# Adding transfers into the result in DRAM in place of loaded partial sums, in a two-layer graph kernel

## What is computed

```python
h = relu(layernorm(x));  h = h @ W0 + B0
mask = (adj < 0.5) & ~eye
S = where(mask, exp(-(1/adj - 1/mu)**2 / (2*sigma**2)), 0)
x = x + S @ h                       # layer 1
h = relu(layernorm(x)) @ W1.T
x = x + (adj*adj + eye) @ h         # layer 2; x is the result
```

## Time and profile before

| | |
|---|---|
| median of 3 runs | 1907.28 us |
| the profiled execution, its own time | 1907.14 us |
| its span, first to last instruction | 1905.3 us |
| TensorE busy | 1850.5 us (97%) |
| VectorE busy | 1732.5 us (91%) |
| ScalarE busy | 1733.1 us (91%) |
| DMA, mean | 521.19 MB, 274 GB/s |
| transfers of GpSimd's queue | 196, 51.39 MB |

### The profile page before, as it was taken

One profiled execution on the slowest core, in us unless ns is written; L12 is line 12 of the kernel. 1 busy time (PEld: TensorE's weight loads), 2 busy tenths in 40 slices (PEclk: granted clock), 3 DMA queues, 4 the chain that ended last, 5 costly groups with the idle time before them and its releaser, 6 DMA issues.

```text
span 1905.3 us, 13395 instructions
## 1 busy us (share of the span) xinstructions
PE 1850.5 (97%) x4820; PEld 886.4 (47%) x4820; DVE 1732.5 (91%) x1024; ACT 1733.1 (91%) x986; POOL 111.6 (6%) x201
## 2 busy tenths in 40 slices
PE   6989999999999999999999999999999999999997
PEld 4544443444444444444444444444444445555554
DVE  7999999998999999999999999999999955678776
ACT  7999999898999999999999999999999988777552
POOL 0000001100000000000000000000000000000112
PEclk9999999999999999999999999999999999999999
DMA  7576887797868687767776686666566577667995
GB/s 264 204 287 255 317 306 278 302 342 284 346 240 337 252 320 283 279 253 276 269 272 241 264 307 238 255 242 231 227 231 226 198 277 279 270 247 302 338 372 229
DMA packets 84289, 521.19 MB, mean 274 GB/s; under 512 B 11008, under 2 KB 11392, under 8 KB 28032
## 3 DMA queue, kind: packets, MB, share of 16 engines
q1 hardware_dynamic: 68544, 468.94, 64.6%
q0 software_dynamic: 15680, 51.39, 7.4%
HBM read 492.50 MB, written 27.79 MB: 273 GB/s over the span
## 4 chain that ended last, share of the span: by engine, by line
PE 31%; DVE 24%; ACT 23%; issue 18%; DMA 3%; POOL 1%; DVEq 0%; POOLq 0%; SPq 0%
PE p_x L483 9%; PE p_l1a L449 9%; DVE rings L624 8%; DVE rings L617 8%; ACT rings L792 7%; ACT rings L797 7%; ACT rings L802 6%; PE p_l1b L449 6%; DVE rings L635 5%; PE p_own L483 4%; ACT rings L810 2%; DMA acc_dram<-xa_buf 1%; DMA outT<-xa_buf 1%; DMA x_buf<-xT 1%; DVE xa_buf L734 1%
## 5 line engine op out<-in xcount | busy, mean ns | idle before, releaser
L624 DVE SCALAR_TENSOR_TENSOR rings<-rings,small 128x2048 f32<-128x2048 f32 x256 | 599.8, 2343 | 24.3 <-ACT rings L797 24.1
L617 DVE SCALAR_TENSOR_TENSOR rings<-rings 128x2048 f32<-128x2048 f32 x256 | 584.4, 2283 | 8.3 <-PE p_l1b L449 7.7
L802 ACT ACTIVATE rings<-rings,small 128x2048 f32<-128x2048 f32 x256 | 533.2, 2083 | 46.2 <-DVE rings L624 45.8
L792 ACT ACTIVATE rings<-rings,small 128x2048 f32<-128x2048 f32 x256 | 509.5, 1990 | 13.7 <-DVE rings L617 9.7
L483 PE MATMUL p_x<-rings,h 128*128 128x512 f32 x1128 | 512.6, 599 | 8.7 <-DVE xa_buf L729 4.8
L797 ACT ACTIVATE rings<-rings 128x2048 f32<-128x2048 f32 x256 | 488.0, 1906 | 5.5
L449 PE MATMUL p_l1b<-rings,h 128*128 128x512 f32 x1024 | 459.7, 595 | 0.0
L449 PE MATMUL p_l1a<-rings,h 128*128 128x512 f32 x1024 | 457.5, 593 | 0.7 <-DVE h L681 0.7
L483 PEld LDWEIGHTS p_x<-rings,h 128*128 128x128 f32 x1128 | 215.5, 192 | 274.7 <-issue 263.2
L635 DVE TENSOR_TENSOR rings<-rings 128x2048 f32<-128x2048 f32 x135 | 308.3, 2284 | 6.6 <-DMA rings<-adjT 3.3
L449 PEld LDWEIGHTS p_l1b<-rings,h 128*128 128x128 f32 x1024 | 195.3, 191 | 243.7 <-issue 241.6
(11 more groups left out here) (95 smaller groups left out, 575.1 us busy)
## 6 DMA issues: line engine op xcount, KB each, us to landing
rings<-adjT SPq DMA_DIRECT2D x439, 1024.0 KB, 6.9
xa_buf<-acc_dram POOLq DMA_DIRECT2D x77, 256.0 KB, 6.5
acc_dram<-xa_buf POOLq DMA_DIRECT2D x74, 256.0 KB, 5.8
x_buf<-xT SPq DMA_DIRECT2D x32, 256.0 KB, 5.4
outT<-xa_buf POOLq DMA_DIRECT2D x16, 256.0 KB, 7.8
acc_dram<-y_buf POOLq DMA_DIRECT2D x15, 256.0 KB, 5.4
y_buf<-acc_dram POOLq DMA_DIRECT2D x13, 256.0 KB, 4.6
acc_dram<-x_buf POOLq DMA_DIRECT2D x1, 256.0 KB, 5.2
```

The source lines that it names most:

```text
L617: dve.scalar_tensor_tensor(out=tile(s_ring, slot_of(t)), in0=tile(a_ring, slot), scalar=CUTOFF, in1=tile(a_ring, slot), op0=ALU.is_lt, op1 ...
L624: dve.scalar_tensor_tensor(out=v, in0=v, scalar=neg_2c, in1=v, op0=ALU.add, op1=ALU.mult).then_inc(squared, 1)
L792: act.activation(v, v, ACT.Ln, bias=tiny_c).then_inc(ln_done, 1)
L802: act.activation(v, v, ACT.Exp, bias=exp_bias, scale=neg_k).then_inc(sens_done, 1)
```

## The change

`acc_dram` and all 90 loads of partial sums are gone. Every store of a row, of a chain or of `y_buf`, goes to `outT` in place. The first one of a row writes; each later one is issued with `accum_op=add`, so that the transfer adds the buffer to what lies in DRAM. It is issued after a wait for the row's previous store (`BEFORE`). VectorE copies each bank of a chain and no longer adds, and `add_y` is one addition instead of two. There were 106 stores (90 of chains, 16 of rows) and 90 loads; there are 106 transfers now, of which 90 add. Buffers, banks, items and the order of the stores stay as they are.

```diff
-EVENTS = sorted([(ch.end + 2, 1, ch.row, ch) for ch in CHAINS if not ch.final]
+EVENTS = sorted([(ch.end + 2 + (S_STEPS if ch.final else 0), 1, ch.row, ch) for ch in CHAINS]
                 + [(NC * (c + 1) + 5, 0, c, None) for c in range(NC)], key=lambda e: e[:3])
+BEFORE, LATEST = {}, {}
+for _, _, row, ch in EVENTS:
+    BEFORE[(row, ch)] = LATEST.get(row)
+    LATEST[row] = (row, ch)
...
             def add_y(c):
                 dve.wait_ge(x1_added, c + 1)
-                if c in PRIORS:
-                    dve.wait_ge(prior_loaded, 16 * (PRIORS.index(c) + 1))
-                    dve.tensor_tensor(y_buf[:, :], y_buf[:, :], x_buf[c % 2][:, :],
-                                      ALU.add).then_inc(prior_added, 1)
-                    dve.wait_ge(prior_added, PRIORS.index(c) + 1)
-                elif c >= 2:
+                if c >= 2:
                     dve.wait_ge(y_stored, 16 * c)
                 dve.wait_ge(q_used, OWN_LAST[c] + 1)
-                dve.tensor_tensor(y_buf[:, :], p_own[c % 2][:, :],
-                                  (y_buf if c in PRIORS else x_buf[c % 2])[:, :],
+                dve.tensor_tensor(y_buf[:, :], p_own[c % 2][:, :], x_buf[c % 2][:, :],
                                   ALU.add).then_inc(y_ready, 1)
...
                 dve.wait_ge(q_used, ch.last_m + 1)
-                if state_before(ch) is None:
-                    if k >= XA_RING:
-                        dve.wait_ge(xa_stored[k % XA_RING], 16 * (k // XA_RING))
-                    dve.tensor_copy(buf[:, :], p_chain[ch.bank][:, :]).then_inc(xa_added, 1)
-                else:
-                    loads = len([o for o in CHAINS[:k + 1]
-                                 if o.index % XA_RING == k % XA_RING and state_before(o) is not None])
-                    dve.wait_ge(xa_loaded[k % XA_RING], 16 * loads)
-                    dve.tensor_tensor(buf[:, :], p_chain[ch.bank][:, :], buf[:, :], ALU.add).then_inc(xa_added, 1)
+                if k >= XA_RING:
+                    dve.wait_ge(xa_stored[k % XA_RING], 16 * (k // XA_RING))
+                dve.tensor_copy(buf[:, :], p_chain[ch.bank][:, :]).then_inc(xa_added, 1)
...
+            def wait_before(row, ch):
+
+                if BEFORE[(row, ch)] is None:
+                    return ALU.bypass
+                _, other = BEFORE[(row, ch)]
+                if other is None:
+                    pool.wait_ge(y_stored, 16 * (row + 1))
+                else:
+                    pool.wait_ge(xa_stored[other.index % XA_RING], 16 * (other.index // XA_RING + 1))
+                return ALU.add
...
             def store_chain(ch):
                 pool.wait_ge(xa_added, ch.index + 1)
-                pool.dma_start(columns(outT if ch.final else acc_dram, ch.row),
-                             xa_buf[ch.index % XA_RING][:, :]).then_inc(xa_stored[ch.index % XA_RING], 16)
+                how = wait_before(ch.row, ch)
+                pool.dma_start(columns(outT, ch.row), xa_buf[ch.index % XA_RING][:, :],
+                               accum_op=how).then_inc(xa_stored[ch.index % XA_RING], 16)
```

More of the change, by code:

```diff
@@ L229 @@
     TRANSFERS.append((ch.store, 0, ch.index))
[L230 to L236, removed]
     ch.after = [o for o in CHAINS[:ch.index] if o.bank == ch.bank]
@@ L246 @@
     TRANSFERS.append((first_item(NC * (c + 1) + 5) + 0.1, 2, c))
-    if c in PRIORS:
-        TRANSFERS.append((first_item(NC * c + 13), 3, c))
 TRANSFERS.sort()
@@ L261, in sem @@
             return ctx.enter_context(nc.semaphore(name))
-        acc_dram = nc.dram_tensor("acc_dram", [D, N], F32).ap()
         h1 = sb("h1", [P, NC * G, D])
@@ L351, in gnn_program @@
         h2_ready = sem("h2_ready")
-        prior_added = sem("prior_added")
         y_ready = sem("y_ready")
         y_stored = sem("y_stored")
-        prior_loaded = sem("prior_loaded")
-        xa_loaded = [sem(f"xa_loaded{n}") for n in range(XA_RING)]
         xa_added = sem("xa_added")
@@ L884, in store_y @@
                     pool.wait_ge(y_ready, c)
-                pool.dma_start(columns(acc_dram, c), (x_buf[0] if c == 0 else y_buf)[:, :]).then_inc(
-                    y_stored, 16)
-            def wait_state(n):
-                _, _, row, ch = EVENTS[n]
-                if ch is None:
-                    pool.wait_ge(y_stored, 16 * (row + 1))
-                else:
-                    pool.wait_ge(xa_stored[ch.index % XA_RING], 16 * (ch.index // XA_RING + 1))
-            def load_prior(c):
-                if c > 1:
-                    pool.wait_ge(y_stored, 16 * c)
-                wait_state(prior_of(c))
-                pool.dma_start(y_buf[:, :], columns(acc_dram, c)).then_inc(prior_loaded, 16)
-            def load_state(ch):
-                if state_before(ch) is None:
-                    return
-                k = ch.index
-                if k >= XA_RING:
-                    pool.wait_ge(xa_stored[k % XA_RING], 16 * (k // XA_RING))
-                wait_state(state_before(ch))
-                pool.dma_start(xa_buf[k % XA_RING][:, :], columns(acc_dram, ch.row)).then_inc(
-                    xa_loaded[k % XA_RING], 16)
+                how = wait_before(c, None)
+                pool.dma_start(columns(outT, c), (x_buf[0] if c == 0 else y_buf)[:, :],
+                               accum_op=how).then_inc(y_stored, 16)
             def store_chain(ch):
                 pool.wait_ge(xa_added, ch.index + 1)
-                pool.dma_start(columns(outT if ch.final else acc_dram, ch.row),
-                             xa_buf[ch.index % XA_RING][:, :]).then_inc(xa_stored[ch.index % XA_RING], 16)
+                how = wait_before(ch.row, ch)
+                pool.dma_start(columns(outT, ch.row), xa_buf[ch.index % XA_RING][:, :],
+                               accum_op=how).then_inc(xa_stored[ch.index % XA_RING], 16)
             for _, kind, n in TRANSFERS:
@@ L919, in _ @@
                     store_chain(CHAINS[n])
-                elif kind == 1:
-                    load_state(CHAINS[n])
-                elif kind == 2:
+                else:
                     store_y(n)
-                else:
-                    load_prior(n)
 def kernel(x, adj, L0_gnn_W, L0_gnn_B, L0_gnn_mu, L0_gnn_sigma, L1_gnn_W):
```

## The result

The changed kernel takes 1900.12 us (median of 12 runs, 1897.27 to 1901.8), the kernel before 1904.84 us in 12 runs beside it. The ratio is 0.9974, 95% interval 0.9967 to 0.9982: 4.7 us faster.

What follows compares the result with a forecast made beforehand. The prediction saw no single bound in layer 1, with TensorE, VectorE and ScalarE full, and full DMA engines in the tail. Terms: -1.0 (rows) - 0.3 (tail) + 1.7 (end) = +0.4 us on 1907.28, so 1907.7 us, range 1901 to 1917.

Steps and rivals of the forecast that it cites:

- one or two of the thirteen: Layer 1 rows: of 13 VectorE additions removed, one or two reach the path: -1.0 us, range -8.9 to 0.
- The prediction's own sign of being wrong: Layer 1: the forecast is wrong if, among other signs, the rows shorten by 0.68 us each.
- Rival B: Rows: VectorE is the bound, all 8.9 us of the removed additions count, 1899.8 us; chance 0.12.
- -0.3: Tail: TensorE's 2.9 us of stalls go, but tile 253 lets VectorE come only 0.3 us earlier with unchanged DMA work.
- an earlier request does not help while the DMA engines are full: Tail: tile 253 comes when it came, at 1875.6 us, since the DMA engines' busy share is about 1.0.
- the prediction's own sum: Tail: ten adding transfers, each dearer than 1.44 us, delay tile 253, less 0.28 us to spare; 2.16 us each gives +6.9.
- The price of adding: DMA engines: an adding transfer takes 1.44 us of all engines, like load and store together, so DMA work stays the same.
- the landing 4.0 forecast: End: the last adding transfer lands after 4.0 us, between 2.3 for a store alone and 5.5 for both in turn.
- Rival C: Tail: dear adding transfers delay tile 253 through full DMA engines; 1916.4 us at three plain stores' price, 1923.6 at four; chance 0.23.
- from 1.6 on: Tail: from 1.6 us of engine time for each adding transfer the kernel is slower than forecast.
- +1.7: End: the last transfer's landing is on the path and grows from 2.3 to 4.0 us; range 0 to +3.2.
- nothing, as forecast: VectorE, chains: 77 additions of 683 ns become copies of 679 ns, 0.3 us in all, taken as 0.

Runs made afterwards that it cites:

- idle_all: The changed kernel with one additional, overwritten VectorE addition of 128x512 in add_y of rows 3 to 15, waiting for no load: 1904.6 us, ratio 0.9994.
- before_ring5: The kernel before with five buffers for the chains in place of four; loads, stores and additions the same: 1904.19 us, ratio 0.9997.
- before_last3_sp: The kernel before with loads and stores of the last three final chains on SyncE's queue, no adding transfer: 1898.12 us, ratio 0.9967.
- extra1: The changed kernel with one additional plain store of 256 KB behind each of the first twelve final stores: 1905.22 us, ratio 1.0.

## Why the prediction was wrong

*VectorE in the rows: the step that failed.* The term -1.0 "one or two of the thirteen" measured -5.1. The prediction took the idle 2.5 us of VectorE in row 12 for slack that takes up the saving, and let it speak for rows 4 to 10, although row 3 had VectorE as the fullest engine. Row 10 has the same 2.5 us and shortened all the same. It also read two waits of 24.5 and 15.8 us over the whole stretch as if both engines had slack. Each is small for 214 steps of three engines in turn, and `idle_all` shows that up to row 10 none of it took up a longer VectorE. The prediction's own sign of being wrong, rows that shorten by 0.68 us each, came true in sum over seven rows. Rival B named this mechanism; its 8.9 us were too many, since the rows from 11 on give nothing. Why the saving stops counting behind row 10 is not shown.

*The tail: the second failed size.* -0.3 was forecast, -3.0 measured between the profiled executions. That the stall goes, and that tile 253 is the next to be late, was right: VectorE waits 0.46 us for it after the change. Wrong was that "an earlier request does not help while the DMA engines are full". The request came 3.7 us earlier and the tile 2.9; in `before_ring5`, with the traffic unchanged, 3.4 us earlier and 1.4. The busy share is 1.0 in kernels whose tile loads land after 7.8 us and after 13.3 us in the median. By the prediction's own sum the measured price of adding would have moved the tail by 10 x (1.73 - 1.44) - 0.28 = +2.6 us. How much of the 3.0 us the waits had, how much the traffic, and how much the one execution of before that was profiled stays open: a kernel with the same loads had 107.2 us (`before_last3_sp`). Open is also why an adding transfer, at 1.73 us of engine time, disturbs the tiles less than two plain ones at 1.4 in sum (106.6 against 108.3 us).

*The price of adding.* 1.44 forecast, 1.73 measured; the landing 4.0 forecast, 4.2 measured: right in kind, the first a fifth above the forecast. Rival C did not come, but it is near: with 0.7 us more for each final chain (`extra1`) the whole gain is gone. That it did not come at 1.73 us, where the prediction has the kernel slower than forecast from 1.6 on, is the tail's failed step again.

*The end.* +1.7 was charged to the landing. That landing is hidden behind GpSimd's drain. Between the profiled executions the end grew by 0.3 us, as much as the last issue (0.86 us where a store took 0.54); but the drain begins with that issue and not behind it, and among all kernels it varies by 6 us, so that no run shows the 0.3 us to be the issue's.

*VectorE, chains, and the queue.* Copies cost 688 ns where 683 were added: nothing, as forecast. Of the waits for a row's previous store one, of 3.9 us on GpSimd's queue, showed in the tail, and nobody waited for it.

Sum of what was measured: -5.1 - 3.0 + 0.3 = -7.8 us between the profiled executions, of whose 8.7 another 0.9 lies before row 1 with nothing changed there. The medians say -4.7 (interval -6.3 to -3.4 by the ratio). Of the 7.6 us between the forecast of 1907.7 and the measured 1900.12, 2.4 are no term of the prediction: it started from the median of three runs, 1907.28, and in twelve runs the kernel before has 1904.84. The other 5.1 are the change, +0.4 against -4.7, and the rows' term alone was 4.1 off. That the remaining terms nearly cancel in the medians proves none of them. The difference of 4.0 us between profiled executions and medians is not explained: the profiled one of before is 2.3 us above its median, and the end, and the tail where chains load their sums, are the stretches that vary.

## What to carry to other kernels

Where three engines are full, an average of idle time over rows or a total of waits does not tell which of them is the bound; put a needless instruction on the engine in question and look at fixed marks, stretch by stretch. One profiled execution is one draw: a wait that stood out in it was absent in another with the same instructions up to there. A busy share of 1.0 of the DMA engines is no proof that requests can't be served sooner: look at how long loads take to land, and at what an additional transfer does. And look at what follows the last issue of each queue: here GpSimd's closing drain cost more than the change gave, and moving three transfers to another queue took the kernel from 1900.1 to 1893.2 us (ratio 0.9974 to 0.9939).

## What the runs showed of the hardware

- GpSimd's DRAIN at its last DMA issue took 3.5 to 9.3 us in these executions, in no order by the kind of the last transfer. With three last transfers on SyncE's queue the program ended 3.2 or 3.3 us after the start of VectorE's last instruction in place of 4.8 to 10.5.
- An adding transfer of 128 x 512 float32 from SBUF into DRAM took 1.73 us of all 16 DMA engines, a plain one 0.68; its issue 0.86 against 0.54 us, its landing with empty engines 4.2 against 2.3 us.
- With one or two additional stores behind each final store in GpSimd's queue the tile loads had 66.4 and 66.6% of the DMA engines' time and moved 16.1 and 16.2 MB in 60 us.
- 1 MB tile loads landed after 7.8 to 13.3 us in the median at busy shares of 0.99 to 1.04.
